# A graph layer on one core: which segments take the end part, and the order of the last eight tiles

## What is computed

```
q, k, v = x @ Wq + bq, x @ Wk + bk, x @ Wv + bv
e = edge_attr @ We
alpha = sum_c(q[dst] * (k[src] + e)) / sqrt(32)
ea = exp(alpha - segment_max(alpha)[dst])
share = ea / (segment_sum(ea)[dst] + 1e-16)
out = segment_sum((v[src] + e) * share) + (x @ Ws + bs)
result = layernorm(x + out)        # every node, edges or none
```

## Time and profile before

| | |
|---|---|
| time, median of 3 runs | 1258.26 us (1256.74 to 1258.81) |
| profiled execution: its time, its span | 1254.81 us, 1253.0 us |
| busy share PE, DVE, POOL, ACT | 96%, 85%, 66%, 56% |
| last slot of the loop with all its work (slot 195) ends | about 1206.4 us |
| from there to the end of the span | 46.6 us |

### The profile page before, as it was taken

One profiled execution on the slowest core, in us unless ns is written; L12 is line 12 of the kernel. 1 busy time (PEld: TensorE's weight loads), 2 busy tenths in 40 slices (PEclk: granted clock), 3 DMA queues, 4 the chain that ended last, 5 costly groups with the idle time before them and its releaser, 6 DMA issues. The chain is left out here.

```text
span 1253.0 us, 26960 instructions
## 1 busy us (share of the span) xinstructions
PE 1207.9 (96%) x7651; PEld 1096.4 (87%) x7651; DVE 1068.5 (85%) x3333; ACT 706.4 (56%) x2263; POOL 825.5 (66%) x747
## 2 busy tenths in 40 slices
PE   7799999999999999999999999999999999999983
PEld 6588888888888888889999999999999889999982
DVE  3789887877878778799999999999999999999983
ACT  2444444555555555556666666666666566666662
POOL 1456656565556656556877778777777777878754
PEclk9899999999999999999999999999999999999996
DMA  6799978778788887843344344444444534444411
GB/s 198 262 293 332 310 277 293 269 265 282 272 281 275 269 285 269 284 166 109 118 119 138 113 136 136 128 150 127 137 137 132 152 118 151 145 129 136 120 57 45
DMA packets 106716, 238.57 MB, mean 190 GB/s; under 512 B 24598, under 2 KB 39114, under 8 KB 106569
## 3 DMA queue, kind: packets, MB, share of 16 engines
q1 hardware_dynamic: 78152, 167.50, 39.9%
q0 software_dynamic: 28416, 69.35, 17.8%
HBM read 156.05 MB, written 88.78 MB: 195 GB/s over the span
## 5 line engine op out<-in xcount | busy, mean ns | idle before, releaser
L532 POOL DMA_INDIRECT rows_in<-xrows_dram,slot x308 | 341.6, 1109 | 85.7 <-issue 82.2
L1135 PE MATMUL bank<-w_y,xT 128*128 128x256 f32 x1568 | 373.2, 384 | 17.2 <-DVEq L752 8.8
L1135 PEld LDWEIGHTS bank<-w_y,xT 128*128 128x128 f32 x1568 | 288.4, 192 | 52.5 <-DVEq L752 8.8
L1155 PE MATMUL bank<-w_kv,sd 128*128 128x512 f32 x1176 | 311.7, 400 | 0.0
L560 POOL DMA_INDIRECT out_dram<-area,where x196 | 220.4, 1124 | 65.1 <-issue 55.3
L626 ACT ACTIVATE square<-y 128x256 f32<-128x256 f32 x392 | 159.8, 409 | 178.4 <-DVE var L833 110.8
L1155 PEld LDWEIGHTS bank<-w_kv,sd 128*128 128x128 f32 x1176 | 210.4, 188 | 37.4
L636 ACT CAST sd<-bank 128x512 fp32r<-128x512 f32 x196 | 115.1, 587 | 188.1 <-PE bank L1147 187.0
L1155 PE MATMUL bank<-w_s,sd 128*128 128x256 f32 x1176 | 190.9, 298 | 0.4 <-DVE area L980 0.4
L523 POOL TENSOR_TENSOR rstd<-var,half 128x4 f32<-128x4 f32 x98 | 111.1, 1133 | 118.8 <-DVE var L833 117.1
L825 DVE TENSOR_TENSOR y<-bank,bias_s 128x512 f32<-128x512 f32 x196 | 134.1, 684 | 64.4 <-PE bank L1135 64.0
(11 more groups left out here) (122 smaller groups left out, 1738.0 us busy)
## 6 DMA issues: line engine op xcount, KB each, us to landing
xT<-xt_dram SPq DMA_DIRECT2D x98, 512.0 KB, 4.6
out_dram<-y SPq DMA_DIRECT2D x98, 512.0 KB, 4.0
eT<-et_dram SPq DMA_DIRECT2D x98, 256.0 KB
dst_all<-dst_row_dram SPq DMA_DIRECT2D x49, 256.0 KB
ahead<-rows_in SPq DMA_DIRECT2D x42, 256.0 KB, 4.8
rows_in<-ahead SPq DMA_DIRECT2D x84, 128.0 KB
rows_in<-xrows_dram,slot POOLq DMA_INDIRECT x392
out_dram<-area,where POOLq DMA_INDIRECT x196
```

What stands on the lines that cost most here:

```text
L532: nc.gpsimd.indirect_dma_start(out=rows_in[:, t % RIN, i, :], out_offset=None, in_=xrows, in_offset=bass.IndirectOffsetOnAxis(ap=slot[:, t ...
L1135: ins = nc.tensor.matmul(node_bank(p)[:, i * D:(i + 1) * D], xT[:, u % RX, c, 2 * b + i, :], w_y[:, c, :], start=(c == 0), stop=(c == KC - 1))
L1155: ins = nc.tensor.matmul(to, rows[a][:, c * P:(c + 1) * P], weights[b][:, c, :], start=(first and n == 0), stop=(last and n == len(terms) ...
```

## The change

Only segments that cross a tile boundary now go through the end part: a tile's scatter leaves out a segment that continues into the next tile, and one whose destination is the last row of the tile before. The end part writes at most one row for each tile's first entry (`rep_i`, 196 entries, two blocks of 98), and `esame` has 196 columns instead of 392. `rep_i` is filled by six new DMAs on SP's queue in slot 8, of 97 or 98 rows with one 4-byte element each. The slot loop of PE, DVE, ACT and POOL stops after slot 195, and the rest (tiles 188 to 195; DRAIN is 188, LAST is group 48) is written out in an order of its own. For tiles from 188 on the messages are made in place in `v`, and one matmul of 32-bit operands replaces the two of float32r parts; `high_mv` and `low_mv` are left out there.

```diff
-        marks = early[:, 0:7 * TILES].rearrange("p (n t) -> p n t", t=TILES)
-        assert 7 * TILES <= LATE * D
-        col_i, end_i, inner = marks[:, 0:2].bitcast(I32), marks[:, 2:4].bitcast(I32), marks[:, 4:7]
+        marks = early[:, 0:5 * TILES].rearrange("p (n t) -> p n t", t=TILES)
+        assert 5 * TILES <= LATE * D
+        col_i, end_i, inner = marks[:, 0:2].bitcast(I32), marks[:, 2].bitcast(I32), marks[:, 3:5]
...
+        rep_i = sb("rep_i", [EW, 3, OB], I32)
...
+        DRAIN = TILES - LAG
-            return (bank[0], bank[1], bank[2], bank[3])[b][0:EW, 0:D]
+            return bank[1 + b][0:EW, 0:D]
+            if t >= DRAIN:
+                return bank[(4, 6, 0, 1, 2)[(t - DRAIN) % 5]][:, 0:D]
...
+                sp.wait_ge(pool_const, 4)
+                firsts, lasts = edge_ends[0], edge_ends[1]
+                for to, of in ((rep_i[:, 0, 0:1], firsts[0:EW]), (rep_i[:, 0, 1:2], firsts[EW:]),
+                               (rep_i[1:, 1, 0:1], lasts[0:EW - 1]), (rep_i[:, 1, 1:2], lasts[EW - 1:TILES - 1]),
+                               (rep_i[:, 2, 0:1], firsts[1:EW + 1]), (rep_i[0:EW - 1, 2, 1:2], firsts[EW + 1:])):
+                    sp.dma_start(to, of.rearrange("(i o) -> i o", o=1)).then_inc(loaded_ent, 16)
...
+            t = scattered_by(TILES - 1)
+            for g in range(LAST - 2, LAST + 1):
+                for u in range(t, g * EG - 1):
+                    scatter(u)
+                t = max(t, g * EG - 1)
+                root(g)
+            for u in range(t, TILES):
+                scatter(u)
             pool.wait_ge(t_var, 1)
-            nc.gpsimd.tensor_tensor(erstd[:], evar[:], half[0:EW, 0:EB], ALU.pow).then_inc(t_rstd, 1)
-            for b in range(EB):
+            nc.gpsimd.tensor_tensor(erstd[:], evar[:], half[0:EW, 0:OB], ALU.pow).then_inc(t_rstd, 1)
+            for b in range(OB):
                 pool.wait_ge(t_rows, b + 1)
                 nc.gpsimd.indirect_dma_start(
                     out=out, out_offset=bass.IndirectOffsetOnAxis(ap=egoto[:, b:b + 1], axis=0),
...
+            square_z(DRAIN - 1)
+            for t in range(DRAIN - 7, DRAIN - 4):
+                normalise(t)
+            weigh(LAST)
+            square_z(DRAIN)
+            square_z(DRAIN + 1)
+            keep_ends(LAST)
+            normalise(DRAIN - 4)
+            normalise(DRAIN - 3)
+            square_z(DRAIN + 2)
+            square_z(DRAIN + 3)
+            act.wait_ge(t_below, 1)
+            nc.scalar.activation(erun, epk, ACT.Exp, scale=SCALE).then_inc(t_p, 1)
+            normalise(DRAIN - 2)
+            normalise(DRAIN - 1)
+            for t in range(DRAIN + 4, TILES):
+                square_z(t)
+            for t in range(DRAIN, TILES):
+                normalise(t)
...
-                    dve.wait_ge(loaded_m, 16 * 3)
+                    dve.wait_ge(loaded_m, 16 * 2)
                     nc.vector.tensor_tensor(inner[:, 0, :], col_i[:, 0, :], col_i[:, 1, :], ALU.is_equal)
                 if n == 1:
-                    nc.vector.tensor_tensor(inner[:, 1, :], col_i[:, 0, :], end_i[:, 0, :], ALU.is_equal)
-                    then(nc.vector.tensor_tensor(inner[:, 2, :], col_i[:, 0, :], end_i[:, 1, :], ALU.is_equal))
+                    nc.vector.memset(inner[:, 1, 0:1], 0.0)
+                    then(nc.vector.tensor_tensor(inner[:, 1, 1:], col_i[:, 0, 1:], end_i[:, 0:TILES - 1], ALU.is_equal))
                 if n == 2:
                     then(nc.vector.tensor_tensor(inner[:, 0, :], inner[:, 0, :], inner[:, 1, :], ALU.max))
-                    then(nc.vector.tensor_tensor(inner[:, 0, :], inner[:, 0, :], inner[:, 2, :], ALU.max))
                     then(nc.vector.scalar_tensor_tensor(out=where[:], in0=inner[:, 0, :], scalar=SKIP, in1=col_f[:],
                                                         op0=ALU.mult, op1=ALU.add))
...
+                    to = v[:, t % RV, :]
+                    if t < DRAIN:
+                        over(dve, mv_low, t - RMV + 1)
+                        to = mv[:, t % RMV, :]
+                    nc.vector.tensor_tensor(heads(to), heads(v[:, t % RV, :]),
                                             wide(share[:, j:EG * H:EG], C), ALU.mult).then_inc(mv_ready, 1)
...
-                t_then(nc.vector.tensor_tensor(enext[:], ent_i[:, 0, :], ent_i[:, 2, :], ALU.is_equal))
-                t_then(nc.vector.scalar_tensor_tensor(out=egoto[:], in0=enext[:], scalar=SKIP, in1=ent_f[:],
+                t_then(nc.vector.tensor_copy(rep_f[:], rep_i[:, 0, :]))
+                t_then(nc.vector.tensor_tensor(enext[:], rep_i[:, 0, :], rep_i[:, 1, :], ALU.not_equal))
+                t_then(nc.vector.tensor_tensor(estays[:], rep_i[:, 0, :], rep_i[:, 2, :], ALU.is_equal))
+                t_then(nc.vector.tensor_tensor(enext[:], enext[:], estays[:], ALU.max))
+                t_then(nc.vector.scalar_tensor_tensor(out=egoto[:], in0=enext[:], scalar=SKIP, in1=rep_f[:],
                                                       op0=ALU.mult, op1=ALU.add))
                 for i in range(EB):
-                    ins = nc.vector.tensor_scalar(esame[i], erow_i[0:EW, :], ent_f[:, i:i + 1], None, ALU.is_equal)
+                    ins = nc.vector.tensor_scalar(esame[i], erow_i[0:EW, 0:ENTRIES:2], ent_f[:, i:i + 1], None,
+                                                  ALU.is_equal)
                 t_then(ins)
...
+            take_q(TILES - 1)
+            values(TILES - 1)
+            products(TILES - 1)
+            scores(TILES - 1)
+            messages(DRAIN + 1)
+            take_z(DRAIN)
+            messages(DRAIN + 2)
+            maximum_before(LAST)
+            maximum_after(LAST)
+            shift(LAST)
+            messages(DRAIN + 3)
+            variance_of(LAST - 2)
+            sum_before(LAST)
+            sum_after(LAST)
+            take_z(DRAIN + 1)
+            keep_den(LAST)
+            invert(LAST)
+            share_out(LAST)
+            for t in range(DRAIN + 4, TILES):
+                messages(t)
+            offsets(LAST - 2)
+            take_z(DRAIN + 2)
+            take_z(DRAIN + 3)
+            entry_step(0)
+            entry_step(1)
+            variance_of(LAST - 1)
+            for t in range(DRAIN + 4, TILES):
+                take_z(t)
+            offsets(LAST - 1)
+            entry_step(2)
+            entry_step(3)
+            variance_of(LAST)
+            dve.wait_ge(t_turned, 1)
+            t_then(nc.vector.tensor_scalar(eden[:], small_b[0:EW, EB * H:2 * EB * H], TINY, None, ALU.add))
+            t_then(nc.vector.reciprocal(erden[:], eden[:]))
+            t_then(nc.vector.tensor_tensor(eshare[:], small_b[0:EW, 0:EB * H], erden[:], ALU.mult))
+            entry_messages(0)
+            entry_messages(1)
+            offsets(LAST)
+            entry_messages(2)
+            entry_messages(3)
+            for b in range(OB):
                 dve.wait_ge(t_summed, b + 1)
                 ins = nc.vector.bn_stats(estats[:, b, :], entry_bank(b))
             t_then(ins)
-            for b in range(EB):
...
+            def root(t):
+                if t < DRAIN:
+                    over(pe, z_copied, t - 1 if t > BOTH else t)
+                if DRAIN <= t < DRAIN + 2:
+                    pe.wait_ge(z_copied, t - 1)
+                if t == DRAIN + 2:
+                    pe.wait_ge(low_ready, TILES)
+                if DRAIN + 3 <= t < DRAIN + 5:
+                    pe.wait_ge(v_ready, TILES - DRAIN - 4 + t - 1)
+                if t >= DRAIN + 5:
+                    pe.wait_ge(z_copied, t - 4)
+                product(z_bank(t), [a[:, 2 + t % RD, :] for a in sd], w_s, True, False)
+            def weighted(t):
+                pe.wait_ge(same_ready, t + 1)
+                if t < DRAIN:
+                    pe.wait_ge(mv_low, t + 1)
+                    nc.tensor.matmul(z_bank(t), same[:, t % RSAME, :], mv_part[0][:, t % 2, :], start=False, stop=False)
+                    nc.tensor.matmul(z_bank(t), same[:, t % RSAME, :], mv_part[1][:, t % 2, :], start=False,
+                                     stop=True).then_inc(z_mm, 1)
+                else:
+                    pe.wait_ge(mv_ready, t + 1)
+                    nc.tensor.matmul(z_bank(t), same[:, t % RSAME, :].bitcast(F32), v[:, t % RV, :], start=False,
+                                     stop=True).then_inc(z_mm, 1)
...
+            root(DRAIN)
+            weighted(DRAIN)
+            root(DRAIN + 1)
+            turn_alpha(LAST)
+            root(DRAIN + 2)
+            root(DRAIN + 3)
+            weighted(DRAIN + 1)
+            root(DRAIN + 4)
+            weighted(DRAIN + 2)
+            weighted(DRAIN + 3)
+            turn_weights(LAST)
+            root(DRAIN + 5)
+            pick_ends()
+            root(DRAIN + 6)
+            root(DRAIN + 7)
+            for t in range(DRAIN + 4, TILES):
+                weighted(t)
...
-            pe.wait_ge(q_copied, TILES)
-            pe.wait_ge(v_ready, TILES)
```

(4 more changed lines are left out.)

79 lines of the change are left out of this document (32 added, 47 removed).

## The result

The changed kernel took **1246.68 us** (median of 6 runs, 1246.31 to 1248.42), where the kernel before took 1258.18 in the same session, that is on the same chip in turn with it (6 runs, 1256.74 to 1258.81): a ratio of 0.9912, with a 95% interval of 0.9899 to 0.9925, so 9.4 to 12.7 us less.

A forecast was written before the change was run, and what follows sets the result against it. TensorE bounds the kernel until slot 195, then a chain across engines behind 1206.4 us. Tail -8.0 and marks +0.3 give -7.7, from the median 1258.26 to 1250.6 us; range 1248.6 to 1253.6.

The forecast's parts named there:

- The tail forecast: Behind 1206.4 us, the chain from the last eight tiles to the last scatter was to change as priced step by step.
- the exp over the entries was to end near 1218.5: Last eight tiles: the new order ends this exp at 1218.5 instead of 1224.4, 5.9 us earlier.
- VectorE was to idle some 2 us at `offsets(47)`: After the exp, VectorE waits about 2 us for GpSimd's root of group 47, queued behind tile 186's scatter.
- the power was to follow five scatters without a gap: End part: GpSimd's five last scatters set the power's start, 1234.55 against 1239.97, with VectorE's variance done over 1 us before.
- my 8.0: Whole tail: the last scatter starts at 1238.4 instead of 1246.37, 8.0 us earlier, with what follows unchanged.
- not 4.8: Entry product on TensorE: two blocks, 14 records instead of 26, leave 4.8 us of 7.62 until the first block is done.
- my +0.3: Entry marks near 1000 us: three added small operations less the shorter `esame` cost +0.3 us, which TensorE waits in full.
- instead of 2.6: Slot 8: the six new loads hold SP's queue for 2.6 us ahead of a load of `xT`.
- the cover: Slot 8: 4.8 us spare in the `xT` loads hides the six new loads; cost 0, bound 1.5 us.
- the two loads of 97 rows use one engine: Slower rival: undivided new loads delay `xT`, stalling 1.6 or 17.8 us, 1268.4 at worst; 5%.
- the last of the sum: Final step: subtracts the 7.7 us gain from before's median 1258.26, 3.45 above its profiled execution, giving 1250.6 us.
- The clock falls earlier: Rival: TensorE's clock drops to 0.50 at 1206, making the following work 5.6 us later, 1256.2 us; 6%.

The follow-up runs named there:

- a_roots: Changed kernel with GpSimd's roots of groups 47 and 48 ahead of the scatters of tiles 186 and 189: 1246.02 us, 0.9918 of before.
- b_same_2: Kernel before, unchanged, profiled once more: 1457.82 us in that execution, in a session where all kernels ran some 200 us longer.
- a_same: Changed kernel, unchanged, run again with a second profile: 1247.25 us, 0.9917 of before.
- b_warm_2: Kernel before with eleven dummy matmuls around the transposes ahead of the entry product, second run: 1255.59 us, 0.9978 of before.
- b_order: Kernel before with only the new order of the last eight tiles and 32-bit sums; four blocks and old marks kept: 1252.32 us, 0.9955 of before.
- b_both_2: Kernel before with the entry marks spread over slots and eleven dummy matmuls around the transposes, second run: 1249.60 us, 0.9933 of before.
- b_warm: Kernel before with eleven dummy matmuls around the transposes ahead of the entry product, first run, long session: 0.997 of before.
- b_both: Kernel before with spread entry marks and eleven dummy matmuls around the transposes, first run, long session: 0.995 of before.
- b_same: Kernel before, unchanged, run as a copy beside itself for a second profile: 1255.88 us, 1.0002 of before.
- b_two: Kernel before with only the two blocks of rows, their six loads and new marks; old order of the last tiles: 1251.38 us, 0.9957 of before.

## Why the prediction was off

**What held.** The tail forecast, point by point: the exp over the entries was to end near 1218.5, or 1219.9 by the 1.4 us by which this profile reaches the tail later, and ended at 1219.56; VectorE was to idle some 2 us at `offsets(47)` behind GpSimd's root, and idled 1.84; the power was to follow five scatters without a gap and did, with the variance done 2.1 us sooner (1234.52 against 1236.58). From the root product at 1206.36 in before and at 1207.72 now, the span's end came 46.64 and 38.88 us later, 7.8 us less against my 8.0. `a_roots` confirms the cause in its profile: with the roots sooner the wait at `offsets(47)` goes and the power comes 1.0 us sooner. Two sizes were off. The power came 0.6 us later than forecast (1236.58, where 1234.55 and the 1.4 make 1235.95), as three of the scatters on the way took 1.24 to 1.58 us and not 0.98; and the product took 5.3 us to the first statistics and not 4.8, which GpSimd hid. The marks cost TensorE 2.3 us of wait instead of 2.0, my +0.3. SP's six loads took 4.07 us instead of 2.6, and the cover held: TensorE is busy in the whole of 150 to 170. By the Trainium skill ("DMA: Bandwidth & Descriptors", section "Why a DMA increments its semaphore by 16 and not by 1") the two loads of 97 rows use one engine; no row here shows how they were divided, only that no stall followed.

**The step that failed** is the last of the sum: "The median of before is 3.45 above its profiled execution; from it the change gives 1258.26 - 7.7". It takes those 3.45 us to be something that every kernel has. The changed kernel doesn't have them: its median lies 1.7 us below its own profiled execution. By the runs they are time lost to TensorE's low clock in an ordinary execution of before, in two places that its profiled execution had escaped. One, the marks, the change leaves. The other, the last tiles and the product behind them, it takes away: that tail is 34.85 us to the power in `b_same_2` against 31.58 in the profile I priced, 3.27 more (2.23 up to the transposes, 1.04 behind them), and no profile with the new order has it.

With that term the sum closes. From `turn_alpha(48)` to the span's end the profiles have 44.61 and 37.04, 7.57 less; 3.27 more for the long tail; 0.3 back at the marks, where the clock then falls in both: 10.5 us, where 9.4 to 12.7 were measured, and 8.8 to 12.2 for the copy `a_same`. Each side by itself closes less well. The profiled execution of before was 0.8 us late at 561 against the mean of the others; less that, with 1.3 for the marks and 3.27 for the tail, before comes to 1258.6 (measured 1258.18). That of the changed kernel was 0.5 late and had the fall at the marks already, which makes 1247.9 (measured 1246.68, and 1247.25 in `a_same`). So about 1 us of the 11.5 has no cause here. Three other kernels fit. `b_warm_2` against the long tail saves 34.85 - 31.98 = 2.9 and gained 1.5 to 4.0; against the short one it would lose 0.4. `b_order` saves 5.8 against the long tail and 2.5 against the short one, and gained 4.0 to 7.4. `b_both_2` saves 34.85 - 29.56 = 5.3 against the long tail and 3.3 at the marks (2.0 of wait, 1.3 for the clock), 8.6 in all, and gained 8.6. The mean granted clocks fit as well: of 13 runs of before in the session of `b_warm_2`, ten had 0.983 or 0.984 and took 1257.2 to 1259.4, where the profiled execution above had 0.988 and took 1254.81; none of 29 runs of kernels with the new order, in the sessions of ordinary length, was below 0.987.

I had the mechanism in hand, as the rival "The clock falls earlier", but looked for it only in the new tail. The earlier trace rows showed a clock of 0.50 in the old one, and TensorE's waits of 1.5 us there were in the trace; that a clock which falls on one side of a row of matmuls in one execution may fall on the other in the next was the question to ask of the old kernel too.

**What stays open.** That ordinary executions of before have the long tail is inferred. It rests on one profile of it, in a session in which the slots ahead took longer, on three profiles with the dummies at the product (`b_warm` and `b_both` in such a session, `b_warm_2` in one of ordinary length), and on the medians and mean clocks of runs without a profile. The clocks of before's runs in the session of the result itself aren't recorded. The direct test by median, dummies in the last tiles, fell into long sessions both times. How often before has the long tail seems to differ from session to session: in those of `b_same`, `b_two` and `b_warm_2`, 5 of 15, 7 of 9 and 10 of 13 of its runs had a clock of 0.983 or 0.984, and its medians were 1256.1, 1257.3 and 1258.2. Nor did I settle what decides, in a given execution, on which side of `pick_ends` the clock is low.
